# Transposing one form of the layer norm's result instead of two, and the feed-forward's first layer as three rounded products, in a fused attention and feed-forward block

## What is computed

```python
xn = layernorm(x)                                   # no gain, eps 1e-5
# attention, 16 heads of 64
h  = rmsnorm(xn, norm_w)
q, k, v = h @ Wq, h @ Wk, h @ Wv
q, k = q/|q| * (q_gamma+1)*8, k/|k| * (k_gamma+1)*8 # per head
p  = softmax(tanh(q @ k.T / 50) * 50 / 8)
a  = (p @ v) @ Wo
# feed-forward, hidden 512; m1, m2 are rank-4 products of 16 rows of xn, new for each batch
f  = gelu(xn @ (W1 + scale*m1).T + b1) @ (W2 + scale*m2).T + b2
out = x + a + f
```

## Time and profile before

| | us |
|---|---|
| median of 3 runs | 1065.68 (1064.24 to 1067.22) |
| profiled execution | 1069.78 |
| its span | 1067.6 |
| PE matmul busy | 1033.9 (97%) |
| POOL (GpSimd) busy | 981.2 (92%) |
| ACT (ScalarE) busy | 976.3 (91%) |
| DVE (VectorE) busy | 938.0 (88%) |
| DMA, mean of 16 engines, transposes of heads included | 43% |
| mean granted TensorE clock | 0.995 |

### The profile page before, as it was taken

How to read it: one execution, slowest core, us unless ns; L and a number is a source line. 1 busy time by engine, 2 the same in 40 slices (tenths; PEclk the granted TensorE clock), 3 DMA queues, 4 the chain that set the end, 5 groups by cost and what they waited for, 6 DMA issues and landing times.

```text
span 1067.6 us, 34237 instructions
## 1 busy us (share of the span) xinstructions
PE 1033.9 (97%) x12889; PEld 844.5 (79%) x12889; DVE 938.0 (88%) x2217; ACT 976.3 (91%) x1417; POOL 981.2 (92%) x912
## 2 busy tenths in 40 slices
PE   6689999999999999999999999999999999999997
PEld 4468888888888888888888888888888888888877
DVE  5888999989999989999988999988999998999972
ACT  3689999999999999999999999999999999999996
POOL 6699999999999999999999999999999999999883
PEclk9899999999999999999999999999999999999999
DMA  3244434444453345544445444345444444444451
GB/s 117 46 86 73 90 81 73 76 87 82 85 81 80 72 84 86 82 82 76 83 76 87 84 80 81 72 86 90 79 82 82 77 78 90 77 86 73 72 99 31
DMA packets 310492, 85.44 MB, mean 80 GB/s; under 512 B 282021, under 2 KB 309817, under 8 KB 310329
## 3 DMA queue, kind: packets, MB, share of 16 engines
q1 hardware_dynamic: 310328, 83.25, 42.8%
HBM read 11.09 MB, written 4.19 MB: 14 GB/s over the span
## 4 chain that ended last, share of the span: by engine, by line
PE 43%; POOL 27%; issue 9%; SPq 6%; DVE 6%; ACT 4%; DMA 4%; POOLq 0%; ACTq 0%
POOL probs_lo L1014 11%; PE ps_scores L526 9%; PE ps_y L574 5%; PE ps_aux L501 4%; POOL sq_k L995 4%; POOL halves L1006 4%; PE ps_o L552 4%; PE ps_aux L512 4%; PE ps_aux L446 4%; DMA heads_T<-halves 3%; SPq L411 3%; PE ps_y L572 3%; PE ps_aux L448 3%; PE ps_aux L447 3%; SPq L399 2%
## 5 line engine op out<-in xcount | busy, mean ns | idle before, releaser
L1014 POOL TENSOR_TENSOR probs_lo<-probs 128x1024 f16<-128x1024 f32 x256 | 485.1, 1895 | 20.0 <-ACT probs L619 18.7
L612 ACT ACTIVATE clamped<-ps_scores 128x1024 f32<-128x1024 f32 x256 | 265.4, 1037 | 44.3 <-PE ps_scores L526 37.1
L619 ACT ACTIVATE probs<-clamped 128x1024 f32<-128x1024 f32 x256 | 272.8, 1066 | 3.0 <-PE ps_o L554 0.4
L552 PEld LDWEIGHTS ps_o<-v_hi,probs 128*128 128x128 bf16 x2048 | 183.9, 98 | 57.3 <-issue 53.0
L526 PE MATMUL ps_scores<-heads_T 64*128 64x256 f16 x3072 | 212.5, 271 | 5.3 <-ACT clamped L612 3.1
L552 PE MATMUL ps_o<-v_hi,probs 128*128 128x65 bf16 x2048 | 214.8, 195 | 2.8 <-POOL probs_lo L1014 1.6
L553 PE MATMUL ps_o<-v_lo,probs 128*128 128x64 bf16 x2048 | 212.4, 193 | 0.0
L554 PE MATMUL ps_o<-v_hi,probs_lo 128*128 128x65 bf16 x2048 | 211.8, 194 | 0.0
L446 PE MATMUL ps_aux<-w_hi,xhT_hi 128*128 128x512 f32 x384 | 176.1, 459 | 13.5 <-DVE qk L824 9.1
L553 PEld LDWEIGHTS ps_o<-v_lo,probs 128*128 128x128 bf16 x2048 | 187.8, 99 | 0.0
L554 PEld LDWEIGHTS ps_o<-v_hi,probs_lo 128*128 128x128 f16 x2048 | 187.7, 97 | 0.0
(11 more groups left out here) (85 smaller groups left out, 2001.8 us busy)
## 6 DMA issues: line engine op xcount, KB each, us to landing
heads_T<-halves SPq DMA_TRANSPOSE x512, 2.5
x_in<-in_L_attn_tokens_dram SPq DMA_DIRECT2D x32, 128.0 KB, 2.4
x_res<-in_L_attn_tokens_dram SPq DMA_DIRECT2D x32, 128.0 KB, 2.3
out_dram<-y_sb SPq DMA_DIRECT2D x32, 128.0 KB, 2.0
sel_raw<-xn SPq DMA_DIRECT2D x192, 4.0 KB
qk<-in_L_attn_Wkv_dram SPq DMA_DIRECT2D x2, 512.0 KB, 5.6
qk<-in_L_attn_Wq_dram SPq DMA_DIRECT2D x1, 512.0 KB, 3.6
qk<-in_L_ffn_W_dram SPq DMA_DIRECT2D x2, 256.0 KB
```

The costliest lines, as they stand in the source:

```text
L552: pe.matmul(full, hi[:, col], v_hi[:, par, u, h], start=(u == 0), stop=False)
L612: nc.scalar.activation(clamped[:].rearrange("p j n -> p (j n)"), ps_scores[:].rearrange("p j n -> p (j n)"), ACT.Tanh).then_inc(clamp_done, 1)
L619: nc.scalar.activation(probs[:, pair % RING].rearrange("p j n -> p (j n)"), clamped[:].rearrange("p j n -> p (j n)"), ACT.Exp, bias=LIFT, ...
L1014: g.tensor_tensor(probs_lo[:, buf].rearrange("p j n -> p (j n)"), probs[:, buf].rearrange("p j n -> p (j n)"), probs[:, buf].rearrange("p ...
```

## The change

- GpSimd makes only xn; xh and its multiplication go. PE makes two transposes in slot 1 instead of four, ScalarE makes one rounded copy (xhT_hi, now of xn) and no float32 copy xnT; both transposed parts are kept for three batches instead of two.
- q and k are normalised anyway, so the missing RMS factor cancels; only the floor under their squared lengths is scaled by it (norm_floor, made on GpSimd), and the seed's first instruction is split in two halves with a column operand each.
- v gets the RMS factor when it is read: ScalarE's v_hi becomes an ACTIVATE with a column operand as scale, VectorE's v_lo a scalar_tensor_tensor with the same operand.
- The two sums var_eps move from GpSimd to VectorE (slot 4), with a reciprocal and a product of two small SBUF tiles behind them, between the statistics and the scaling of q0. GpSimd keeps the power.
- hid0 and hid1 are made with mm3: twelve float32r products of 256 columns. For that ScalarE rounds w1_eff (w1_hi) in slot 2, between tanh and the copy of oT1, and GpSimd makes the rest (w1_lo) in slot 2, before probs_lo.

The diff, cut (buffers, semaphores and indices of the three-deep buffers are left out):

```diff
-    [("half", 3), ("tanh",), ("oT", 1, -1), ("exp",), ("oT", 2, -1)],
+    [("half", 3), ("tanh",), ("w1_hi",), ("oT", 1, -1), ("exp",), ("oT", 2, -1)],
...
-    [("bias",), ("hi", 7, 0), ("lo",)],
+    [("bias",), ("hi", 7, 0), ("w1_lo",), ("lo",)],
...
@@ PE, xT and hid
-                        pe.transpose(bank[:, t * P:(t + 1) * P], xh[:, t], ident[:])
-                    for t in range(TT):
-                        ins = pe.transpose(bank[:, seq + t * P:seq + (t + 1) * P], xn[:, par, t], ident[:])
+                        ins = pe.transpose(bank[:, t * P:(t + 1) * P], xn[:, par, t], ident[:])
...
                     if k == 0:
-                        wait(pe, weff_made, 2 * b + 1)
+                        wait(pe, w1_lo_made, b + 1)
                     for j in range(2):
-                        ins = pe.matmul(bank[:, j * seq:(j + 1) * seq], w1_eff[:, 2 * k + j], xnT[:, b % 3],
-                                        start=True, stop=True)
+                        c = 2 * k + j
+                        ins = mm3(bank[:, j * seq:(j + 1) * seq], w1_hi[:, c], w1_lo[:, c], xhT_hi[:, b % 3], xhT_lo[:, b % 3])
...
@@ ScalarE
+            def w1_round(st):
+                b, _, _ = st.batch(0)
+                act.wait_ge(weff_made, 2 * b + 1)
+                nc.scalar.copy(w1_hi[:], w1_eff[:]).then_inc(w1_hi_made, 1)
...
-                    nc.scalar.copy(xhT_hi[:, par], bank[:, 0:seq])
-                    nc.scalar.copy(xnT[:, b % 3], bank[:, seq:2 * seq]).then_inc(xnT_copied, 1)
+                    nc.scalar.copy(xhT_hi[:, b % 3], bank[:, 0:seq]).then_inc(xT_rounded, 1)
...
-                    nc.scalar.copy(v_hi[:, par, t, 8 * c:8 * c + 8, 0:DH],
-                                   bank.rearrange("p (h d) -> p h d", d=DH)).then_inc(v_hi_made, 1)
+                    nc.scalar.activation(v_hi[:, par, t, 8 * c:8 * c + 8, 0:DH],
+                                         bank.rearrange("p (h d) -> p h d", d=DH), ACT.Copy,
+                                         scale=rstd[:, b % 4, 1, t:t + 1]).then_inc(v_hi_made, 1)
...
@@ VectorE, norm_var
+                dve.wait_ge(meanvar_made, 2 * b + 2)
+                wait(dve, floor_made, b)
+                v.tensor_scalar(var_eps[:, 0], mean_var[:, :, 1], LN_EPS, None, ALU.add).then_inc(vareps_made, 1)
+                v.tensor_scalar(ms_eps[:], mean_var[:, :, 1], 1.0 + RMS_EPS, RMS_EPS * LN_EPS,
+                                ALU.mult, ALU.add).then_inc(vareps_made, 1)
+                dve.wait_ge(vareps_made, 2 * b + 2)
+                v.reciprocal(inv_eps[:], var_eps[:, 0]).then_inc(inveps_made, 1)
+                dve.wait_ge(inveps_made, b + 1)
+                v.tensor_tensor(var_eps[:, 1], ms_eps[:], inv_eps[:], ALU.mult).then_inc(ratio_made, 1)
...
@@ VectorE, seed and v_lo
-                    v.tensor_scalar(minus_half_norm2, norm2[:], NORM2_MIN, -0.5, ALU.max, ALU.mult)\
-                        .then_inc(seed_made, 1)
+                    dve.wait_ge(floor_made, b + 1)
+                    half_of = TT * HEADS
+                    for t in range(TT):
+                        part = slice(t * half_of, (t + 1) * half_of)
+                        v.tensor_scalar(minus_half_norm2[:, part], norm2[:, part], norm_floor[:, b % 4, t:t + 1], -0.5,
+                                        ALU.max, ALU.mult).then_inc(seed_made, 1)
...
-                    v.tensor_tensor(v_lo[:, par, t, 8 * c:8 * c + 8], bank.rearrange("p (h d) -> p h d", d=DH),
-                                    v_hi[:, par, t, 8 * c:8 * c + 8, 0:DH], ALU.subtract).then_inc(v_split, 1)
+                    v.scalar_tensor_tensor(v_lo[:, par, t, 8 * c:8 * c + 8], bank.rearrange("p (h d) -> p h d", d=DH),
+                                           rstd[:, b % 4, 1, t:t + 1], v_hi[:, par, t, 8 * c:8 * c + 8, 0:DH],
+                                           ALU.mult, ALU.subtract).then_inc(v_split, 1)
...
                 elif kind == "low":
                     dve.wait_ge(aux_filled["low"], 2 * b + k + 1)
+                    if k == 0:
+                        wait(dve, w1_lo_made, b)
...
@@ GpSimd
-                g.tensor_scalar(var_eps[:, 0], mean_var[:, :, 1], LN_EPS, None, ALU.add).then_inc(vareps_made, 1)
-                g.tensor_scalar(var_eps[:, 1], mean_var[:, :, 1], 1.0 + RMS_EPS, RMS_EPS * LN_EPS,
-                                ALU.mult, ALU.add).then_inc(vareps_made, 1)
...
+                g.tensor_scalar(norm_floor[:, b % 4], var_eps[:, 1], NORM2_MIN, None, ALU.mult).then_inc(floor_made, 1)
...
-                g.tensor_tensor(xh[:], x_mid[:], rstd[:, 1].unsqueeze(2).to_broadcast([P, TT, P]), ALU.mult)\
...
+            def w1_rest(st):
+                b, _, _ = st.batch(0)
+                pool.wait_ge(w1_hi_made, b + 1)
+                wait(pool, aux_filled["hid"], 2 * b)
+                g.tensor_tensor(w1_lo[:], w1_eff[:], w1_hi[:].bitcast(F32), ALU.subtract).then_inc(w1_lo_made, 1)
```

More of the change, by code:

```diff
@@ L198, in block_kernel @@
         var_eps = sb("var_eps", [P, 2, TT])
-        rstd = sb("rstd", [P, 2, TT])
+        ms_eps = sb("ms_eps", [P, TT])
+        inv_eps = sb("inv_eps", [P, TT])
+        rstd = sb("rstd", [P, 4, 2, TT])
+        norm_floor = sb("norm_floor", [P, 4, TT])
         xn = sb("xn", [P, 2, TT, P])
-        xh = sb("xh", [P, TT, P])
         x_mid = sb("x_mid", [P, TT, P])
-        xnT = sb("xnT", [P, 3, seq])
-        xhT_hi = sb("xhT_hi", [P, 2, seq], F32R)
-        xhT_lo = sb("xhT_lo", [P, 2, seq], F32R)
+        xhT_hi = sb("xhT_hi", [P, 3, seq], F32R)
+        xhT_lo = sb("xhT_lo", [P, 3, seq], F32R)
         qk = sb("qk", [P, 2, TT, QK])
@@ L238, in block_kernel @@
         w1_eff = sb("w1_eff", [P, HC, P])
+        w1_hi = sb("w1_hi", [P, HC, P], F32R)
+        w1_lo = sb("w1_lo", [P, HC, P], F32R)
         w2_eff = sb("w2_eff", [P, 2, HC, P])
@@ L274, in block_kernel @@
         seed_made = sem("seed_made")
+        ratio_made = sem("ratio_made")
+        inveps_made = sem("inveps_made")
+        floor_made = sem("floor_made")
         newton_step = sem("newton_step")
@@ L299, in block_kernel @@
         weff_made = sem("weff_made")
+        w1_hi_made = sem("w1_hi_made")
+        w1_lo_made = sem("w1_lo_made")
         gelu_done = sem("gelu_done")
@@ L488, in aux @@
                     tok, col = slice(t * P, (t + 1) * P), slice(c * 512, (c + 1) * 512)
-                    ins = mm3(bank, xhT_hi[:, par, tok], xhT_lo[:, par, tok], w_hi[:, col], w_lo[:, col])
+                    ins = mm3(bank, xhT_hi[:, b % 3, tok], xhT_lo[:, b % 3, tok], w_hi[:, col], w_lo[:, col])
                 elif kind == "v":
@@ L632, in aux @@
                 act.wait_ge(aux_filled[kind], PER_BATCH[kind] * b + k + 1)
+                if kind == "v" and k == 0:
+                    act.wait_ge(rstd_made, b + 1)
                 if kind == "xT":
-                    nc.scalar.copy(xhT_hi[:, par], bank[:, 0:seq])
-                    nc.scalar.copy(xnT[:, b % 3], bank[:, seq:2 * seq]).then_inc(xnT_copied, 1)
+                    nc.scalar.copy(xhT_hi[:, b % 3], bank[:, 0:seq]).then_inc(xT_rounded, 1)
                 elif kind == "q":
@@ L668, in run @@
                                 exp(st, s)
+                        elif what == "w1_hi":
+                            if "attn" in st.stages:
+                                w1_round(st)
                         elif what == "half":
@@ L940, in norm_apply @@
                 pool.wait_ge(mid_made, b + 1)
-                g.tensor_tensor(xn[:, par], x_mid[:], rstd[:, 0].unsqueeze(2).to_broadcast([P, TT, P]), ALU.mult)
-                g.tensor_tensor(xh[:], x_mid[:], rstd[:, 1].unsqueeze(2).to_broadcast([P, TT, P]), ALU.mult)\
+                g.tensor_tensor(xn[:, par], x_mid[:], rstd[:, b % 4, 0].unsqueeze(2).to_broadcast([P, TT, P]), ALU.mult)\
                     .then_inc(xn_made, 1)
@@ L1032, in run @@
                                 lo_part(st, s)
+                        elif what == "w1_lo":
+                            if "attn" in st.stages:
+                                w1_rest(st)
                         elif what == "hi":
```

20 lines of the change are left out of this document (11 added, 9 removed).

## The result

The changed kernel takes 1198.2 us (median of 6 runs, 1188.1 to 1210.0) against 1065.0 (1063.9 to 1068.4) for the one before: a ratio of 1.1236 with a 95% interval of [1.1204, 1.1269], which leaves out the slowest run (1210.0) as over 1.5% above the fastest. It is slower, as I had thought likeliest, but by 133 us and not by 7: far outside my range of 1055 to 1083.

What follows compares the result with a forecast made beforehand. ScalarE and PE were taken as equally long up to v3, with little spare at oT3. Terms of +0.17 and +0.06 gave +0.23 us a batch, times 31 = +7 us: 1073, with an 8 in 10 range of 1055 to 1083.

Steps and rivals of the forecast that it cites:

- A lock in slot 4: VectorE's new product waits for GpSimd's halves: q0's scaling late by 0.72 + 0.42 us, v1 by about 0.4.
- rival (c): VectorE's product waits for GpSimd in slot 4, delaying v1: 1080, or 1100 with a full wait; chance 0.11.
- tanh(3) to v3: ScalarE's stretch before v3 on PE grows by 0.17 us a batch, from 15.2 to about 15.4 us.
- v_hi with its column scale: ScalarE's v_hi takes 0.08 to 0.09 us more each, a mean of about 680 ns.
- twelve products of 256 columns: PE's float32r hidden layer takes 12 x 0.125 = 1.5 us, 0.3 less than before; bounds 1.4 and 2.8 us.
- w1_hi: ScalarE's rounding copy of 512 columns in slot 2 takes 0.52 to 0.58 us, 0.47 start to start.
- oT3 behind tanh(2): PE stalls about 0.32 us at oT3, as ScalarE's copy of oT1 starts 0.47 us later.
- w1_lo: GpSimd's new slot 2 instruction takes 1.04 us, with 1.6 us to spare before hid0; counted at nothing.
- (a): PE's own list decides, ScalarE regaining elsewhere what it loses: -0.55 us a batch, 1049, or 1057 with half; chance 0.24.
- (b): Gains and losses cancel within 0.3% (1062.5 to 1068.9): column operand costs 0.03 or w1_eff's copy is half hidden; chance 0.20.
- (d): On PE, float32r products of 256 columns pace as those of 512: hidden layer +1.0 us, 1097; chance 0.05.
- The table reload: ScalarE's copy with a column scale might make it load a table again; given no weight.

Runs made afterwards that it cites:

- the kernel without the lock: Changed kernel with the sum as a tensor_reduce, the reciprocal kept and the ratio made by one small GpSimd instruction: 1078.5 us, 1.0111.
- unlocked with the float32 hidden layer: The kernel without the lock, with the earlier float32 hidden layer: xnT copied again, no w1_hi, w1_lo or split products; 1060.9 us, 0.9941.

## Why the prediction was wrong, point by point

**Where the 133 us went.** The change without its lock costs 12 us (1078.5 against 1066.1). The other 120 come with the small instructions on VectorE. By the batch of 34.81 us at full clock, against a quiet period of 32.00 in the kernel without the lock, the wait costs 2.8 us a batch, 87 in 31 batches. What is left, 33 us in the median run, goes with the clock: 37.49 - 34.81 = 2.7 us in a batch with the same wait. In the profiled execution 46 are left (1210.0 - 1077.4 - 87); 15 batches restart v1 at half clock, at 2.7 us each, and in six more from 250 us on the clock falls for a shorter stretch, and they take 35.9 to 36.8 us, about 1.6 more than 34.8: some 50 us in all. This split is a subtraction and a comparison of batches, not an experiment of its own.

**The step that failed** is "A lock in slot 4", the price of rival (c). The mechanism, its place and the wait of v1 that would show it were right; its chance of 0.11 and its size of 1080 to 1100 were not. Three parts of it were wrong:
- Who waits. I let only the product of two tiles wait. The sum with one tensor input waits as well (one sum alone: 16 us). The evidence stood in the earlier trace rows, an instruction of VectorE with one tensor input at 2025 instead of 783 ns; I mentioned it in passing and didn't draw the conclusion that the two sums are instructions of that same kind.
- How long. I took the end of the one GpSimd instruction running, 0.42 us more, at most 1.03. But ends of GpSimd instructions were passed over where the next one followed without a gap, and three of the four instructions can wait one after the other. GpSimd's list was busy for 30.2 of 31.7 us and the halves and probs_lo stand back to back, so in nearly every batch the four were done only with probs_lo: one wait of 3.15 us, up to 4.0, or 1.3 and then 1.9. With the measured 2.8 a batch of standstill on top of the 7 for the rest, the sum would have been 1066 + 7 + 87 = 1160.
- What follows. I priced the standstill of PE as lost time alone; the lower clock, up to some 6 us from v1 on, was in none of my cases.

I had also used only half of a rule. The Trainium skill ("SBUF — State Buffer", section "SBUF: two separate sides") names two kinds of VectorE instruction that exclude GpSimd and are excluded by it: those in a two-port mode and, against a GpSimd instruction that reads SBUF, those with two SBUF inputs. By the Trainium skill's "VectorE: DVE Perf Modes" (sections "What auto-detection actually checks" and "The perf-mode tier table") an instruction with a single source gets that mode if source and destination are both in SBUF and their outermost dimensions are both even or equal (two elements here), tensor_scalar among them; a PSUM operand rules it out, and tensor_reduce has no such mode. Each of these agrees with the runs: the sums wait, the product waits, the tensor_reduce and the tensor_scalar to PSUM don't. Read whole, the rule would have made the first sum of the four wait, which is issued where q0's scaling stood, at 510.91, in the middle of the halves. That section of the Trainium skill has the pair held "for the whole instruction", and the measurement goes beyond that: 3.15 us cover parts of three GpSimd instructions.

**The forecast's own terms,** read on the kernel without the lock:

| term | forecast | measured |
|---|---|---|
| tanh(3) to v3 | 15.4 us | 582.28 - 566.93 = 15.35 |
| v_hi with its column scale | 680 ns | 693 (595 in the earlier trace rows) |
| twelve products of 256 columns | 1.5 us | 569.05 - 567.53 = 1.52 |
| w1_hi | 0.52 to 0.58 us | 0.61; start to start 0.51 |
| oT3 behind tanh(2) | +0.32 us | 2.07 against 1.74: +0.33 |
| w1_lo | 1.04 us | 1.27 |
| quiet period | 31.77 + 0.23 = 32.00 | 32.00 |

They hold but for w1_lo, and the kernel takes 12 us more, not 7. The rest is mostly a term that I put at nothing, GpSimd's lateness ahead of hid0. I gave w1_lo 1.6 us to spare; in seven batches that was used up, and hid0 waits 0.1 to 0.9 us for it, 4.3 us in all. One of them, GpSimd and PE (the view names ScalarE, but w_lo ends 0.15 us ahead of hid0 here, and 0.14 or 0.15 in all seven):

```profile
662.07 1.05 POOL L1036 TENSOR_TENSOR halves<-qk,rnorm_sb 128x512 f16<-128x512 f32 x1 [1.46 <-DMA heads_T<-halves]
663.08 1.26 POOL L1044 TENSOR_TENSOR w_lo<-w_eff,w_hi 128x512 fp32r<-128x512 f32 x1
...
664.49 0.36 PE L454 MATMUL ps_aux<-xhT_hi,w_hi 128*128 128x256 f32 x1 [0.80 <-ACT oT L665]
```

In each of the seven GpSimd had waited 0.8 to 1.5 us for a DMA transpose of heads ahead of its halves, and w1_lo stands behind them. The waits are not there when w1_hi and w1_lo are gone (unlocked with the float32 hidden layer).

**The rivals.** (a), PE's own list decides, came in no version: the fastest has 31.60 us a batch and 1060.9 us, 0.17 us a batch less than before and not 0.55 or half of it. In the change itself ScalarE and the lock forbid it. (b) and (d) are out: the terms are there, and 256 columns cost half of 512 (start to start 0.12 us). The table reload didn't show: v_hi is 98 ns longer, about what the gelu's column operand costs.

**What stays open.** Why the clock falls in some batches and not in others: v1 restarted at half clock after 2.73 us of standstill in one batch, and at full clock after 2.82 in another, and after 3.1 us in batches of the kernel before with the four instructions. And why VectorE gets in between two GpSimd instructions in one batch and not in the next: the sum issued at 719.29 and the one at 569.19 came 0.80 and 0.77 us after the first half had started, and ended after 1.29 and 3.15 us. What alone bounds the period of 31.60 us is open too.

## What to carry to other kernels

An instruction of 0.17 us on VectorE isn't cheap because it is small: where GpSimd is nearly always busy, a tensor_scalar or tensor_tensor between SBUF tiles can wait for several GpSimd instructions in a row, and everything queued behind it waits too; before moving such work, look for a gap in GpSimd's timeline at that place, or give it a form that doesn't wait. A single odd maximum in a min/median/max row (783 against 2025 ns) is to be followed up by looking at what the other engines did at that moment. Slack is to be held against the late batches and not the quiet one: 1.6 us for w1_lo looked ample and were used up in seven batches. And a cost that hits the bounding engine with a standstill can have a second price in its clock.

## What the hardware showed that I had not expected

- Of VectorE's small instructions next to a busy GpSimd, tensor_scalar from SBUF to SBUF (up to 4.0 us) and tensor_tensor of two SBUF tiles (up to 3.2) wait; reciprocal (up to 168 ns) and tensor_reduce (156 to 161 ns) from SBUF to SBUF don't, nor does a tensor_scalar from SBUF to PSUM (L768 of the changed kernel, 243 to 254 ns in 64 instances).
- A waiting VectorE instruction ended within 0.08 us of the end of a GpSimd instruction, in all the traces here. It could pass over up to three such ends where GpSimd went on without a gap (4.0 us), or get in at one (17 of 30 first sums); no trace shows a pause passed over. A wait added to GpSimd won 92 us.
- With a standstill of about 2.8 us TensorE's granted clock was 0.50 for some 6 us from v1 on in about half of the batches (15), at a price of 2.7 us a batch; in others, and after up to 3.3 us, v1 restarted at full clock.
- GpSimd's subtraction with a float32r result took 1.27 us for 512 columns, a float32 multiplication of the same size 1.04.
